# A four-layer attention network with a routed FFN on one core: the content copies on SyncE's queue go behind the exchange, and GpSimd's rotation moves one place in its order

## The reference, cut to what matters

```python
q, k, v = sh(xn @ Wq.T + bq), sh(xn @ Wk.T + bk), sh(xn @ Wv.T + bv)
scores = einsum('bhqd,bhkd->bhqk', q, k)
r = _pos_emb(S)                                    # sines and cosines
rel = einsum('bhqd,ld->bhql', q + u[None, :, None, :], r)
scores = (scores + _rel_shift(rel, S, S)) * HEAD_DIM ** (-0.5)
p = softmax(where(mask, NEG, scores))
```

## Time and profile before

| | |
|---|---|
| time, median of 3 runs | 2368.07 us (2365.6 to 2368.84) |
| the profiled execution's own time | 2368.84 us |
| its span, first to last instruction | 2366.9 us |
| outside the span | 1.9 us |
| TensorE matmul busy | 2278.0 us, 96% of the span |
| VectorE / ScalarE / GpSimd busy | 2006.9 / 1835.7 / 1142.2 us (85 / 78 / 48%) |
| one slot of the layers in the middle | 15.3 us |
| mean granted TensorE clock | 0.991 of full |

### The profile page before, as it was taken

One profiled execution on the slowest core, in us unless ns is written; L12 is line 12 of the kernel. 1 busy time (PEld: TensorE's weight loads), 2 busy tenths in 40 slices (PEclk: granted clock), 3 DMA queues, 4 the chain that ended last, 5 costly groups with the idle time before them and its releaser, 6 DMA issues. The chain is left out here.

```text
span 2366.9 us, 83085 instructions
## 1 busy us (share of the span) xinstructions
PE 2278.0 (96%) x31360; PEld 1972.4 (83%) x31360; DVE 2006.9 (85%) x4943; ACT 1835.7 (78%) x2869; POOL 1142.2 (48%) x2089
## 2 busy tenths in 40 slices
PE   4999999999999999999999999999999999799998
PEld 3788888888888888888888888888888888677776
DVE  6899999988888888888888888888888885677774
ACT  2688888888888888888888888888888888555554
POOL 4555555555544455555445555454555543333332
PEclk8999999999999999999999999999999999899999
DMA  4444333333333333333333333333333331010100
GB/s 136 108 117 109 108 93 92 90 85 88 92 90 98 93 92 85 88 93 87 94 93 97 85 89 87 91 93 91 91 105 91 89 91 38 21 28 28 28 23 19
DMA packets 227431, 196.04 MB, mean 83 GB/s; under 512 B 29024, under 2 KB 225760, under 8 KB 227040
## 3 DMA queue, kind: packets, MB, share of 16 engines
q1 hardware_dynamic: 227040, 190.73, 30.0%
HBM read 14.46 MB, written 4.19 MB: 8 GB/s over the span
## 5 line engine op out<-in xcount | busy, mean ns | idle before, releaser
L995 DVE TENSOR_REDUCE rowmax<-bank 128x4 f32<-128x1024 f32 (+1 forms) x768 | 916.0, 1220 | 107.6 <-PE bank L572 75.2
L813 ACT ACTIVATE probs<-bank 128x1024 f32<-128x1024 f32 x768 | 737.5, 1024 | 84.1 <-PE bank L632 83.5
L632 PE MATMUL bank<-qstack,kstack 64*128 64x128 f32 (+1 forms) x4096 | 423.1, 299 | 5.1 <-DMA qstack<-maxrows 5.1
L572 PE MATMUL bank<-kstack,qstack 62*128 62x256 f32 (+1 forms) x4096 | 417.5, 301 | 9.2 <-DMA qstack<-base 9.2
L854 ACT ACT_TABLE_LOAD x256 | 328.4, 1283 | 4.5
L572 PEld LDWEIGHTS bank<-kstack,qstack 62*128 62x128 f32 x4096 | 316.9, 193 | 9.6 <-issue 9.6
L632 PEld LDWEIGHTS bank<-qstack,kstack 64*128 64x128 f32 x4096 | 315.3, 192 | 6.2 <-DMA qstack<-maxrows 6.2
L1169 POOL CAST xn1T_parts<-xn1T 128x256 fp32r<-128x256 f32 x128 | 50.7, 396 | 482.6 <-ACT xn1T L821 482.6
L594 PE MATMUL bank<-maskT_half,pick_half 64*128 64x128 bf16 (+1 forms) x3072 | 267.9, 241 | 10.8 <-DVE turn_c L964 2.2
L721 PE MATMUL bank<-w,hidden 128*128 128x128 f32 x2048 | 273.6, 278 | 2.6 <-ACT hidden L863 2.6
L652 PE MATMUL bank<-probs,v_pad 128*32 128x256 f32 x4096 | 271.1, 382 | 0.6 <-DVE v_tok L976 0.6
(11 more groups left out here) (153 smaller groups left out, 5293.8 us busy)
## 6 DMA issues: line engine op xcount, KB each, us to landing
qstack<-base SPq DMA_DIRECT2D x768, 128.0 KB, 2.4
kstack<-base SPq DMA_DIRECT2D x384, 128.0 KB, 2.5
turn_x<-turn_c SPq DMA_DIRECT2D x512, 32.0 KB, 1.9
qstack<-maxrows SPq DMA_DIRECT2D x256, 16.0 KB
out<-ot SPq DMA_DIRECT2D x16, 256.0 KB, 2.4
h_all<-in_x SPq DMA_DIRECT2D x7, 512.0 KB, 4.4
xin<-in_x SPq DMA_DIRECT2D x14, 256.0 KB, 3.1
w<-in_w SPq DMA_DIRECT2D x8, 256.0 KB, 3.1
```

What stands on the lines that cost most here:

```text
L572: last = pe.matmul(bank[:, b0 + b, i * wide:(i + 1) * wide], qstack[rows, r, p0 + i, t * 128:(t + 1) * 128], kstack[rows, r, p0 + i, 0:wid ...
L632: last = pe.matmul(bank[:, b0 + b, i * wide:(i + 1) * wide], kstack[rows, r, p0 + i, kt * 128:(kt + 1) * 128], qstack[rows, r, p0 + i, q0: ...
L813: act.activation(probs[:, k], bank[:, A_BANK[k]:A_BANK[k] + 2, :], ACT.Exp, scale=SCALE).then_inc(exp_done[k], 1)
L995: dve.tensor_reduce(rowmax[:, n % 2, t, :, p0:p0 + heads], bank[:, M_BANK[k]:M_BANK[k] + 2, :].rearrange("p b (h c) -> p b h c", h=heads), ...
```

## The change

Two moves. On SyncE, `content(s)` leaves its place ahead of `exchange(s)` and is called as `content(s - 1)` at the head of the next slot. Slot ends are not barriers on SyncE, so the queue's order goes from turned_content(s-1), maxima(s-3), content(s), exchange(s), weight loads to content(s-1), turned_content(s-1), maxima(s-3), exchange(s), weight loads. On GpSimd, `turned` leaves its place behind `xn2_split` of the next slot and is called as `turned(s)` at the end of the same slot, behind `xn1_split(s + 1)`; prefill (slot 0), split_w1(0) (slot 4) and split_qkv come after it.

```diff
             for s in SLOTS:
                 if live(s - 1):
+                    content(s - 1)
+                if live(s - 1):
                     turned_content(s - 1)
                 if live(s - 3):
                     maxima(s - 3)
-                if live(s):
-                    content(s)
                 if live(s):
                     exchange(s)
                 loads_behind(s)
@@ gpsimd
                 if live(s - 6):
                     xn2_split(s - 6)
-                if live(s - 1):
-                    turned(s - 1)
                 if s in (N + 4, N + 5):
@@
                 if live(s + 1):
                     xn1_split(s + 1)
+                if live(s):
+                    turned(s)
                 if s == 0:
                     prefill()
```

## The result

The changed kernel takes 2379.78 us (median of 5 runs, 2377.12 to 2389.59), the kernel before beside it 2366.84 (5 runs, 2365.56 to 2368.84): ratio 1.0067, 95% interval 1.0046 to 1.0089. The forecast was 2369.2 with a range up to 2378. The profiled execution took 2385.99 with a span of 2384.0, against 2368.84 and 2366.9 before, so 17.1 us of difference lie open in the traces. It and two further executions of the change on record (2386.41 and 2386.91) are not in the median.

What follows compares the result with a forecast made beforehand. TensorE, busy 494.3 of 500 us in the layers, was taken as the bound. Maxima -2.4, layer starts +6.0 and start -2.5 summed to +1.1 us, giving 2369.2 on the median of 2368.07, range 2362.5 to 2378.

Steps and rivals of the forecast that it cites:

- the price of content behind a load: SyncE: content lands 2.5 us after issue; a load ahead takes issues of some 0.6 us off 2.4 us of cover.
- the term of the start: Pipeline fill: earlier exchange and rotation shorten TensorE's stalls, -2.5 us taken, ends 0 and -3.8.
- the exchange and the first stall: Start: exchange goes out at about 16.2 instead of 19.75, and TensorE's 29.52 becomes 26.5.
- the ordinary slot: GpSimd, steady slot: xn2T's split comes 2.0 us later within 2.54 of slack, leaving 0.5, so it costs nothing.
- the six waits: TensorE waits for xn2T's split, three slots with split_w1 at 1.36 and three behind split_qkv at 0.62: +6.0 us.
- the maxima: TensorE's four waits for maxima in the layers all go: -2.4 us, bounds 0 and -2.4.
- Rival 4: Start gains nothing, layer starts cost in full, 2375.0; or a further low-clock stretch, 2374.2; chance 0.12.
- The clock: Start: TensorE at 1.2 GHz from 56.2 to 66.4 us, 2.4 GHz from then on; 0 put in the sum.
- rival 2: Start gains more: clock rises a stretch earlier, 2364.6, or with the larger advance 2363.3; chance 0.20.

Runs made afterwards that it cites:

- The half on GpSimd alone: Kernel before with only GpSimd's turned moved behind xn1_split in the same slot, SyncE's order as before: 2449.18 us, ratio 1.0351.
- one swap on SyncE: Kernel before with exchange issued ahead of content, both ahead of the loads, GpSimd's order as before: 2363.49 us, ratio 0.9989.
- the version that beats both: Changed kernel with content directly behind exchange, ahead of the loads, and split_w1 and split_qkv moved ahead of xn1_split: 2362.07 us, ratio 0.9975.
- the last run with loads on ScalarE's queue: Changed kernel with loads issued from ScalarE's queue only once SyncE has issued the slot's exchange: 2385.83 us, ratio 1.0081.

## Why the prediction was wrong, by its own steps

- **Failed: the price of content behind a load.** The step said that content "has landed ... with the 2.5 of its kind", and that "where a weight or x load now goes out ahead of it, one or two issues of some 0.6 us come off" the cover. The 2.5 is the median of 384 copies, nearly all in slots without a load, and it is still the median after the change. The last copies of eight of the nine units that ScalarE waits for landed 4.5 to 8.1 us after issue (the longest in unit 4, 82.86 to 90.96); the ninth, unit 0, has no load ahead and took 2.4. The load was priced by SyncE's time (0.58 us) and not by its 512 KB on the DMA engines.
- **So failed: the term of the start**, -2.5, which came out at +8.1 and +4.3 in the two traces of the change, and the term that the sum did not have, the load slots and the experts' slot (+4.5 and +8.1). With content ahead of the loads the start is worth -3.72, between the -2.5 taken and its bound of -3.8; since the start differs by about 1 us between executions, this doesn't tell the two apart.
- **Held: the exchange and the first stall**, 26.48 against 26.5 forecast.
- **Held: the ordinary slot.** Distance 0.65 against 0.55, no waits. The half on GpSimd alone shows how near the edge this is.
- **Held: the six waits**, 5.71 and 5.75 against 6.0.
- **Nearly held: the maxima**, -2.85 against -2.4. The list of waits gives a matmul's own wait, and in the six slots above a slot lost more than its matmul's bracket showed; it may be the same here, which was not taken apart.
- **Rivals.** Rival 4 named the mechanism, ScalarE's split waiting for content in the start and in slots with loads, but priced it with issues, and so gave 2375.0 where 2379.8 and 2386.0 were measured, with a chance of 0.12. The start trace was the place to see it: in the kernel before, the DMA engines' share there was already 0.48, and 0.34 in the layers.
- **Missed, small:** slot 128, below, and some 0.8 us thinly spread, which stay unexplained.
- **The clock.** The prediction read one stretch at the lower level, 56.2 to 66.4 us. The trace of the kernel before has another at the start, from 42.6 to 52.8, and three more in the drain, so "2.4 GHz from then on" is too much. The rival that a higher clock makes the start shorter (rival 2) did not come: it was 0.83 over the first 100 us after and 0.90 before. With content ahead of the loads it was 0.88, and the start gained 3.72 all the same. What the clock costs by itself can be read in the drain, from TensorE's FFN product of slot 132 to that of slot 133, in the kernel before, the change, and the kernel with content ahead of the loads:

```profile
2017.69:2028.03 10.34, 7.00 (x34) 6.33 (x35) 4.53 (x18) 5.30 (x10) 4.55 (x7) 0.67 0.00 1
...
2034.75:2045.10 10.35, 7.01 (x35) 6.34 (x35) 4.53 (x18) 5.30 (x10) 4.55 (x7) 0.67 0.00 1
...
2018.51:2026.15 7.64, 4.41 (x35) 4.00 (x35) 3.87 (x14) 5.11 (x10) 4.03 (x7) 1.00 0.00 1
```

  The same work takes 2.7 us less at the full clock. Eight of the experiments' traces have it so, the kernel before and both traces of the change don't. The eight share no edit, so this belongs to the execution and not to the kernel.
- **Why the loads' cost varies, as far as the traces tell.** Two things vary. One is content's landing: ScalarE's wait behind the same load of x in slot 13 is 1.45 us in one trace of the change and 2.63 in the other. The other is the clock behind the stall. In the experts' slot of the change and of the kernel with its loads on ScalarE's queue, ScalarE waits 3.72 and 3.75 us for content, and TensorE's two waits are 1.07 and 1.32 us in the one and 1.10 and 1.32 in the other. But the slot costs 2.47 and 4.07. These are the windows from where TensorE starts again:

```profile
1761.50:1765.00 3.50, 3.50 (x44) 3.32 (x45) 2.69 (x8) 3.14 (x4) 0.00 (x0) 1.00 0.62 162
...
1746.10:1749.60 3.50, 3.46 (x31) 3.21 (x32) 2.36 (x6) 2.76 (x3) 0.00 (x0) 0.56 0.61 160
```

  The granted clock stays at 1.00 in the first and falls to 0.56 in the second, 44 matmuls against 31, and this is the 1.6 us between them. So a stall costs TensorE its own length, and in some executions a slower stretch behind it. The whole times go along: the slowest run of the change (2389.59) had a mean granted clock of 0.987, the fastest (2377.12) 0.993.
- **Open:** why the same load delays content by more in one execution than in another, and why the clock falls behind a stall in one and not in the next. Runs of the change spread over 12.5 and 10.2 us, those of the kernel before over 7 at most. No run here tells how the DMA engines share between load and content.

## What to carry to other kernels

When a copy changes places in a queue with a load, ask what bytes now go ahead of it and how busy the DMA engines are in that very stretch; the issue time and the median landing say nothing about it, and moving the load to another engine's queue at the same moment doesn't help, while another moment does: behind content, or so early that the load has landed when content goes out. A move that takes two edits on two engines is to be priced, and run, as each half too: here the good part was one swap on SyncE (-0.11%), and with the GpSimd order and the weight splits moved as well it was -0.25%. And a slack spent in every slot (2.59 us down to 0.65) is a debt that the rare slots with extra work pay at once.

## What the hardware showed unexpectedly

In slot 128, VectorE's small instructions take longer when GpSimd's moved rotation runs beside them. VectorE's timeline before, then after with GpSimd's beside it:

```profile
1961.27 0.17 DVE L1005 CAST maxparts<-rowmax 128x32 fp32r<-128x32 f32 x1
1961.48 0.19 DVE L1007 TENSOR_TENSOR maxparts<-rowmax,maxparts 128x32 fp32r<-128x32 f32 x1
1961.59 0.60 DVE L941 TENSOR_SCALAR xn<-h_all,mv,rstd 128x128 f32<-128x128 f32 x2
```

```profile
1977.42 0.73 POOL L1187 TENSOR_TENSOR rotated<-turn_s,turn_x 128x256 f32<-128x256 f32 x1 [2.11 <-issue]
1977.55 0.64 DVE L1005 CAST maxparts<-rowmax 128x32 fp32r<-128x32 f32 x1
1978.23 0.43 DVE L1007 TENSOR_TENSOR maxparts<-rowmax,maxparts 128x32 fp32r<-128x32 f32 x1
1978.58 1.00 DVE L941 TENSOR_SCALAR xn<-h_all,mv,rstd 128x128 f32<-128x128 f32 x2
1978.70 0.81 POOL L1193 TENSOR_TENSOR base<-rotated,base 128x256 fp32r<-128x256 f32 x1
```

The first cast, 0.17 alone, ends at 1978.19, 0.04 after GpSimd's instruction (1978.15). The Trainium skill, page "SBUF — State Buffer", section "Who interferes with whom", says that VectorE and GpSimd share one pair of ports, that a cast of VectorE's can enter a mode that takes this pair, and that whoever issues first has it for the whole instruction while the other stands; this row agrees. Eight traces have both the rotation and the exchange moved. In five of them (the change, its repetition, the change with the splits moved, the version that beats both, and the last run with loads on ScalarE's queue) the rotation meets the cast, which takes 0.63 or 0.64 us, and the slot costs TensorE 0.74. In the other three the rotation starts 0.9 us or more behind the cast's end, the cast takes 0.17, and the slot costs nothing. So it is the meeting of the two instructions, and not the new order by itself, that costs the 0.74.
